# Attention on one core: first loads of three head groups moved into the step loop, and another order of the maxima tiles

## What is computed

```
xn = layernorm(x)
q = (xn @ wq.T).reshape(b, s, 4, 4, 16)
k, v = (xn @ wk.T), (xn @ wv.T)         # reshaped to (b, s, 4, 16)
att = softmax(causal(einsum('bsgmd,btgd->bgmst', q, k) / 4))
ctx = einsum('bgmst,btgd->bsgmd', att, v).reshape(b, s, 256)
out = x + ctx @ wo.T + expert_mixture(xn)
```

## Time and profile before

| | |
|---|---|
| median of 3 runs | 3020.6 us (3019.86 to 3024.7) |
| the profiled execution | 3016.38 us |
| its span | 3014.6 us |
| from the first instruction of attention to its last score tile | 209.2 to 1967.3 us |
| busy in the span | TensorE 88%, VectorE 69%, ScalarE 54%, GpSimd 14% |

### The profile page before, as it was taken

One profiled execution on the slowest core, in us unless ns is written; L12 is line 12 of the kernel. 1 busy time (PEld: TensorE's weight loads), 2 busy tenths in 40 slices (PEclk: granted clock), 3 DMA queues, 4 the chain that ended last, 5 costly groups with the idle time before them and its releaser, 6 DMA issues. The chain is left out here.

```text
span 3014.6 us, 48833 instructions
## 1 busy us (share of the span) xinstructions
PE 2666.1 (88%) x16291; PEld 1591.6 (53%) x16291; DVE 2082.6 (69%) x5148; ACT 1615.0 (54%) x3282; POOL 413.7 (14%) x458
## 2 busy tenths in 40 slices
PE   4854999999999999999999999977697978979999
PEld 2432444444444444444444444356585867869999
DVE  6865888888888889988888988551525431226665
ACT  2530767767776777776677777762534541112221
POOL 1231110010011001100100110124031330011000
PEclk9985999999998999998999999998898988989999
DMA  4999031133033123303321000041422316756654
GB/s 132 321 269 116 7 41 22 25 42 42 5 44 40 21 28 42 42 10 38 42 27 21 7 7 5 9 163 56 146 70 111 125 49 196 216 176 196 195 194 145
DMA packets 191591, 259.50 MB, mean 86 GB/s; under 512 B 66820, under 2 KB 138632, under 8 KB 189864
## 3 DMA queue, kind: packets, MB, share of 16 engines
q1 hardware_dynamic: 170632, 237.17, 31.9%
q10 hardware_dynamic: 20768, 19.93, 2.1%
HBM read 155.16 MB, written 100.70 MB: 85 GB/s over the span
## 5 line engine op out<-in xcount | busy, mean ns | idle before, releaser
L633 ACT ACTIVATE att_pr<-att_ring 128x512 f32<-128x512 f32 (+3 forms) x2560 | 1176.8, 546 | 543.5 <-PE att_ring L714 537.2
L660 DVE TENSOR_REDUCE att_mx<-att_ring 128x1 f32<-128x512 f32 x1536 | 947.7, 681 | 103.6 <-PE att_ring L727 101.5
L727 PE MATMUL att_ring<-att_ks,att_qs 48*128 48x512 f32 (+3 forms) x2560 | 902.5, 443 | 56.3 <-DMA att_v<-v_rows 35.2
L714 PE MATMUL att_ring<-att_qs,att_ks 64*128 64x512 f32 (+3 forms) x2560 | 794.0, 417 | 30.2 <-DMA att_ks<-w_ones 26.3
L714 PEld LDWEIGHTS att_ring<-att_qs,att_ks 64*128 64x128 f32 x2560 | 420.8, 193 | 580.5 <-DVE att_mx L660 277.6
L753 PE MATMUL att_acc<-att_pr,att_v 128*32 128x512 f32 (+3 forms) x5120 | 624.5, 561 | 2.2 <-ACT att_cT L640 1.5
L727 PEld LDWEIGHTS att_ring<-att_ks,att_qs 48*128 48x128 f32 x2560 | 429.9, 195 | 236.0 <-ACT att_pr L633 147.6
L666 DVE CUSTOM_DVE_ANT_0 att_junk<-att_ring,w_causal 128x128 bf16<-128x128 f32 (+3 forms) x1024 | 458.5, 488 | 110.0 <-PE att_ring L727 74.7
L620 POOL TENSOR_SCALAR_AFFINE_SELECT att_pr<-att_pr 128x512 f32<-128x512 f32 x256 | 162.4, 634 | 1565.1 <-ACT att_pr L633 1565.1
L1173 ACT CAST com_e1h<-com_tp 128x1024 fp32r<-128x1024 f32 x64 | 64.5, 1014 | 262.8 <-PE com_tp L1246 236.6
L970 PE MATMUL dis_lp<-dis_y,dis_lg 128*128 128x257 f32 x512 | 119.5, 398 | 83.9 <-ACT dis_lg L857 83.9
(11 more groups left out here) (140 smaller groups left out, 2933.9 us busy)
## 6 DMA issues: line engine op xcount, KB each, us to landing
slot_exps<-dis_e SPq DMA_DIRECT2D x64, 512.0 KB, 2.6
com_e<-slot_exps SPq DMA_DIRECT2D x64, 512.0 KB, 3.5
att_qs<-q_parts SPq DMA_DIRECT2D x96, 256.0 KB, 12.1
q_parts<-proj_part SPq DMA_DIRECT2D x32, 512.0 KB, 3.8
att_ks<-k_parts SPq DMA_DIRECT2D x96, 128.0 KB, 12.8
y_rows<-proj_y SPq DMA_DIRECT2D x16, 512.0 KB, 4.3
y_cols<-proj_yT SPq DMA_DIRECT2D x16, 512.0 KB, 5.1
context<-att_cn SPq DMA_DIRECT2D x64, 128.0 KB, 2.2
```

The source lines that it names most:

```text
L633: nc.scalar.activation(pr[:, s % NPR, h, off:CH], ring[:, bank_of["s", s, h], off:CH], ACT.Exp, scale=float(HD) ** -0.5).then_inc(exp_done, 1)
L660: nc.vector.tensor_reduce(dst, ring[:, bank, :], AX.X, ALU.max).then_inc(mb_used, 1)
L714: nc.tensor.matmul(ring[:, bank_of[e], off:CH], ks[r, g, kb * P:(kb + 1) * P], qs[r, g, c, hf * CH + off:(hf + 1) * CH], start=True, stop= ...
L727: nc.tensor.matmul(ring[:, bank_of[e], 0:wd], qs[r, g, c, q0:q0 + P], ks[r, g, j * CH:j * CH + wd], start=True, stop=True).then_inc(mb_rea ...
```

## The change

Three things are done. The maxima of a chunk get a new order: the heads 1 and 3 make one list and 0 and 2 the other; in each the diagonal tiles are spread evenly among the full ones, widest first in one list and with the halves swapped in the other; the two lists are then interleaved. SyncE loads only head group 0 ahead of the loop; groups 1, 2 and 3 come ahead of the program of the steps 0, 20 and 60, each with its ones. The semaphore for the ones is split in four, and TensorE waits for a group's ones in that group's own first step. GpSimd waits for its memsets once more before its first mask.

```diff
-    MAXES = [(c, h, t, j) for c in range(CPB) for t in range(TPC) for j in range(c + 1) for h in (1, 0, 3, 2)]
+    def chunk_maxes(c, rg):
+        heads = [h for h in range(GS) if h % NRG == rg]
+        full = [(c, h, t, j) for t in range(TPC) for h in heads for j in range(c)]
+        diag = [(c, h, t, c) for t in (3, 0, 2, 1) for h in heads]
+        if rg == 0:
+            diag = diag[len(diag) // 2:] + diag[:len(diag) // 2]
+        n = len(full) + len(diag)
+        at = {(2 * i + 1) * n // (2 * len(diag)) for i in range(len(diag))}
+        full, diag = iter(full), iter(diag)
+        return [next(diag) if k in at else next(full) for k in range(n)]
+
+    MAXES = [x for c in range(CPB) for pair in zip(chunk_maxes(c, 1), chunk_maxes(c, 0)) for x in pair]
...
+    FIRST_LOADS = {0: 1, 20: 2, 60: 3}
...
+        ones_set = [sem(f"ones_set{g}") for g in range(NKV)]
...
-                for g in range(NKV):
+                def load_first(g):
                     load(0, g)
                     for rg in range(NRG):
                         for hl in range(2):
                             row = RG * rg + KR + hl
                             sp.dma_start(ks[row:row + 1, g, :].bitcast(F32),
-                                         w["ones"][0:S // 64, :].bitcast(F32)).then_inc(ones_set, 16)
-
+                                         w["ones"][0:S // 64, :].bitcast(F32)).then_inc(ones_set[g], 16)
+
+                load_first(0)
                 for s in ALL_STEPS:
+                    if s in FIRST_LOADS:
+                        load_first(FIRST_LOADS[s])
                     for e in program(s):
...
+                for g in range(1, NKV):
+                    pool.wait_ge(zeroed[g], 2 * NRG)
...
-                                if n < NBG:
-                                    pe.wait_ge(ones_set, 16 * 2 * NRG * NKV)
+                                if bg < NKV and c == 0:
+                                    pe.wait_ge(ones_set[g], 16 * 2 * NRG)
```

More of the change, by code:

```diff
@@ L547, in attend @@
         c_out = [sem(f"c_out{c}") for c in range(CPB)]
-        (ones_set, sT_ready, exp_done, mask_done, pv_done, mb_ready, mb_used, m_step, nm_ready,
+        ones_set = [sem(f"ones_set{g}") for g in range(NKV)]
+        (sT_ready, exp_done, mask_done, pv_done, mb_ready, mb_used, m_step, nm_ready,
          cT_ready, rz_ready) = (
-            sem(n) for n in ("ones_set", "sT_ready", "exp_done", "mask_done", "pv_done", "mb_ready",
+            sem(n) for n in ("sT_ready", "exp_done", "mask_done", "pv_done", "mb_ready",
                              "mb_used", "m_step", "nm_ready", "cT_ready", "rz_ready"))
```

## The result

The changed kernel takes 2956.69 us (median of 4 runs, 2954.26 to 2959.28), the kernel before 3022.65 beside it; the ratio is 0.978 with a 95% interval of 0.976 to 0.980. The forecast was 2960, in a range of 2932 to 2988. The profiled execution has a span of 2952.4 us against 3014.6, 62.2 less.

A forecast was written before the change was run, and what follows sets the result against it. Attention steps were taken as bound by a chain of TensorE and ScalarE, plus VectorE's lag at maxima transposes, a 26.3 us start wait and low clock. Terms -25.5 + 14 - 29 - 20 = -60.5 gave 2960 us, range 2932 to 2988.

The forecast's parts named there:

- First loads: Start of attention: TensorE's 26.3 us wait for ones goes; gain 25.5 us, bounds 20 to 27.
- Where the loads go: At u24 of the first two groups, late loads delay maxima rows: two 5.3 us stalls plus low clock, 14 us lost.
- Order of the maxima: Chunk ends: VectorE lags less at the transposes of maxima, net 1.8 us a group, 29 us gained.
- counted by the ring: Score tiles waiting for VectorE: u1 loses 0.3 us, u7 0.2, u16 0.1; u1 to u3 win 0.1 to 0.2 back.
- Clock: Low-clock stretches in attention: with u4 shorter, about half of 43 us goes; 20 us gained, bounds 0 and 43.
- sum: Whole kernel: -25.5 + 14 - 29 - 20 = -60.5 us, profiled execution from 3016.4 to 2956.
- a low clock that goes altogether: Attention groups: all 43 us of low clock go, -86 us in total, 2934 us; chance 0.17.
- a clock that stays: Attention groups: low clock stays as frequent as it was, -40 us in total, 2980 us; chance 0.19.
- an order that does nothing: Transposes of maxima: VectorE is late from three short operations, not the mix; -11.5 us, 3009 us; chance 0.09.
- Rival 4: Attention steps: VectorE becomes the bound of the ring, score tiles wait 0.26 us in 25 of 40 steps; 3113 us, chance 0.05.

The follow-up runs named there:

- loads-only kernel: The changed kernel with the old order of the maxima, the moved first loads kept: 3014.15 us, ratio 0.9968 to the kernel before.
- the pair with narrow and wide ends: Kernel before, old loads: lumped maxima with narrowest tiles last, 2942.68 us, 0.9725; even spread with widest diagonal tiles last, 2996.15 us, 0.9913.
- narrow-last kernel: The kernel before with old loads and lumped order, query tiles taken as 1, 2, 3, 0: 2942.68 us, ratio 0.9725.

## Why the prediction was right, point by point

- **First loads**, 25.5 us forecast: the first score tile came 23.7 us earlier, in a run whose attention began 2.0 us later. From each run's own beginning of attention it is 25.8. Right; the loads-only kernel shows it again (25.1).
- **Where the loads go**, 14 us lost: two stalls of 5.3 us were forecast, and 11.3 us were measured for the two (10.1 in the loads-only kernel). With them went 5.5 us of low clock, where I had added 3.5 net: 16.8 against 14. The queue's order as the cause is shown by the kernel that moves the load by one step and has no stall left. Group 1's load cost nothing, as said.
- **Order of the maxima**, 29 us: 2.06 us a group at full clock, times 16, is 33. The four steps with an "m" are 0.49, 0.51, 0.61 and 0.62 us shorter at full clock (u4, u20, u24, u32), 2.2 together, where 2.4 were forecast. The mechanism (less lag at the chunk's end) is shown by the pair with narrow and wide ends. One detail was wrong. I had the standing before the "m" of u4 fall from 0.9 to 0.3 us; it nearly stayed, 0.80 on average after 0.86. The timeline of a u4 after, which answers to the earlier trace rows:

```profile
1016.75 0.18 PEld L734 LDWEIGHTS att_ring<-att_qs,att_ks 64*128 64x128 f32 x1 [0.20 <-issue]
...
1018.55 0.17 DVE L717 TENSOR_TENSOR att_nml<-att_nm,att_nml 128x16 fp32r<-128x16 f32 x1
...
1018.88 0.27 PE L753 MATMUL att_ring<-w_ident,att_nml 128*32 128x128 f32 x1 [0.85 <-DVE att_nml L717]
...
1020.60 0.18 PEld L734 LDWEIGHTS att_ring<-att_qs,att_ks 64*128 64x128 f32 x1 [0.62 <-ACT att_pr L653]
```

  The step lasts 3.85 us instead of 4.35, but TensorE also reaches the transpose earlier, since its score tiles wait less for banks, and so stands nearly as long. Of the idle time left, 19.9 us, 12.7 are here; 3.5 are at u20, 3.6 before the first two transposes in the lead, and none at u24 and u32. Of the losses that I had counted by the ring, u7 was there (2.85 us for 2.55 in the medians of the step), u16 was not, and u1 lost 0.02 instead of 0.3; u34 lost 0.17, and u11, u15, u27 and u37 0.1 each, which I had not counted. Steps ahead of an "m" (u3, u23, u31) won 0.2 to 0.3 each, so outside the four the losses and gains nearly cancel.
- **Clock**, half of 43 us to go: 27.5 us are left, 5.5 of them the new ones behind the stalls. So 21 us of the old went, 20 were forecast. That it fits to 1 us is partly luck: it compares one execution of each kernel, and other executions of the kernel before lie between 3000.9 us at a mean clock of 0.940 and 3029.8 at 0.929. And the reason that I gave, a shorter standing in u4, is not the one, since that hardly shrank; the step as a whole did. Nor does low clock always follow a standing at a transpose: four stretches after begin in a u14, which has none, as at 840.6 us, and the longest in the narrow-last kernel, of 20.5 us, begins in a u10. Where the transposes waited for nothing, low clock fell from 129 to 69 us and did not vanish, while other waits grew. Why fewer low stretches follow stays open: no run here varied the standing alone.
- The **sum** of the four in the profiled executions: 60.5 us forecast, 62.2 measured; the terms were off by 1 to 4 us each, partly against each other. The rivals of a low clock that goes altogether (27.5 us of it are left), of a clock that stays, of an order that does nothing, and of VectorE as the bound are out. Rival 4's mechanism does exist, though: it is what ate the gain where the transpose came one step later.

On the Trainium skill's half of the throttled time (TensorE: Matmul & The Clock Gate, HAM oscillation): the rows of before gave a third, 6.1 us for 17. After, two groups with clock 0.98 have one stretch of 3.4 us at the low level each, the one of 102.10 us in a u14 and the one of 101.25 in a u4. All engines in these two stretches, in that order:

```profile
840.60:844.00 3.40, 3.40 (x16) 1.21 (x8) 2.05 (x5) 1.80 (x4) 0.00 (x0) 0.51 0.00 0
```

```profile
1526.60:1530.00 3.40, 3.40 (x18) 1.64 (x16) 2.46 (x7) 1.98 (x5) 0.00 (x0) 0.50 1.05 117
```

The first group is 1.8 us over 100.28, half of its stretch, and the second 1.0, under a third. So neither share holds everywhere in this case; it goes with the step that the low stretch meets.

## What to carry to other kernels

When one engine waits for a reduction over many tiles, order the tiles so that the cheapest come last, right before the wait. Here spreading them evenly with a light end was worth less (0.9816 for 0.9725); moving the wait a step later was worth as much as the spread, with most of the lag moving into the tiles that share the buffers, and nothing on top of the cheap end. When loads are deferred, look not only at when their data are needed but at which small DMA is next in the same queue: here it was held 13 us behind a load that nobody needed for 40 steps more. Put each deferred load right behind the last urgent transfer of its stretch.

## What was not expected

The small DMAs behind a load waited for all of it: 25.0 us from the load's start for a pair of 8 KB each, issued 11.9 us after it. A low-clock stretch of 3.4 us cost between 1.0 us (101.25 against 100.28, in a u4 of the changed kernel) and 1.8 us (102.10 against 100.28, in a u14 of the same kernel); in a u4 of the kernel before it was 1.3 (103.60 against 102.34). So where the stretch falls changes its price within one kernel. And lumping the narrow maxima at the chunk's end was worth more than the change itself: 0.9725 without touching a load.
